# Twelve unread matmuls ahead of each turn of the peaks in a small-head attention

## The reference, cut to what matters

```
# once, beside a mixture of experts (called E here)
attn = softmax(q @ k^T / sqrt(8)); attn_out = attn @ v         # 32 sequences, 128 keys
# six layers, each of them:
xn = adaln(x, ...); x = x + attn(rope(q), rope(k), v, src_mask) @ so_w.T     # 128 keys (SELF)
xn = adaln(x, ...); x = x + attn(rope(q), rope(k), v, ctx_mask) @ co_w.T     # 77 keys (CROSS)
xn = adaln(x, ...); x = x + gelu(xn @ f1.T + b) @ f2.T + b
```

## Time and profile before

| | us |
|---|---|
| median of 3 runs | 8137.16 |
| lowest, highest | 8121.33, 8175.87 |
| the profiled execution, its own time | 8089.43 |
| its span, first to last instruction | 8087.6 |
| TensorE busy | 6666.4 |
| VectorE busy | 4803.6 |
| ScalarE busy | 2813.6 |
| GpSimd busy | 1457.2 |

### The profile page before, as it was taken

How to read it: one execution, slowest core, us unless ns; L and a number is a source line. 1 busy time by engine, 2 the same in 40 slices (tenths; PEclk the granted TensorE clock), 3 DMA queues, 4 the chain that set the end, 5 groups by cost and what they waited for, 6 DMA issues and landing times. The chain is left out here.

```text
span 8087.6 us, 192854 instructions
## 1 busy us (share of the span) xinstructions
PE 6666.4 (82%) x79848; PEld 4741.3 (59%) x79848; DVE 4803.6 (59%) x16890; ACT 2813.6 (35%) x4969; POOL 1457.2 (18%) x1340
## 2 busy tenths in 40 slices
PE   4444578888798888887996998998898898898897
PEld 3333456666575766765774665565565565565565
DVE  6777854455476666665446645646646645645744
ACT  1221134444334111111113544444444444444443
POOL 1114421122112000000002212212212212212211
PEclk7667788999875555556997858758858758858858
DMA  1000000000031000000003323323323323423420
GB/s 31 0 0 3 2 27 1 1 1 1 5 60 40 3 3 3 3 3 23 1 1 73 71 43 69 71 43 69 70 44 69 65 49 64 71 49 62 72 49 14
DMA packets 328291, 268.31 MB, mean 33 GB/s; under 512 B 48649, under 2 KB 323413, under 8 KB 327259
## 3 DMA queue, kind: packets, MB, share of 16 engines
q1 hardware_dynamic: 327387, 255.62, 17.0%
HBM read 177.84 MB, written 76.37 MB: 31 GB/s over the span
## 5 line engine op out<-in xcount | busy, mean ns | idle before, releaser
L325 DVE TENSOR_REDUCE peak<-ps 128x8 f32<-128x1024 f32 (+1 forms) x832 | 853.5, 1028 | 418.2 <-PE ps L228 390.0
L365 ACT ACTIVATE e<-ps 128x1024 f32<-128x1024 f32 (+1 forms) x832 | 850.3, 1022 | 628.7 <-PE ps L260 628.6
L276 PE MATMUL ps<-e,H_vt 128*32 128x128 f32 (+1 forms) x12288 | 722.8, 375 | 12.5 <-issue 9.0
L373 ACT ACTIVATE oT<-ps 128x512 f32<-128x512 f32 x416 | 248.4, 597 | 873.3 <-PE ps L276 873.3
L253 PE MATMUL ps<-shift,own 8*128 8x128 bf16 (+1 forms) x6656 | 460.1, 278 | 54.3 <-DVE shift L337 30.2
L276 PEld LDWEIGHTS ps<-e,H_vt 128*32 128x32 f32 (+1 forms) x12288 | 405.2, 143 | 137.6 <-issue 38.1
L253 PEld LDWEIGHTS ps<-shift,own 8*128 8x128 bf16 (+1 forms) x6656 | 280.5, 134 | 256.6 <-issue 131.3
L260 PE MATMUL ps<-H_q_stack,H_k_stack 49*128 49x128 bf16 (+1 forms) x6144 | 422.8, 278 | 0.0
L284 PE MATMUL ps<-ident,oT 128*128 128x128 f32 x1664 | 401.2, 386 | 15.6 <-ACT oT L373 11.4
L228 PE MATMUL ps<-H_k_stack,H_q_stack 49*128 49x128 bf16 (+1 forms) x6144 | 346.0, 250 | 43.7 <-issue 33.0
L2257 ACT ACTIVATE F_ex<-ps,F_nm 16x77 f32<-16x77 f32 x256 | 81.1, 317 | 824.5 <-DVE F_nm L2168 824.5
(11 more groups left out here) (655 smaller groups left out, 14512.2 us busy)
## 6 DMA issues: line engine op xcount, KB each, us to landing
scratch<-pT SPq DMA_DIRECT2D x480, 128.0 KB, 2.4
H_q_stack<-scratch SPq DMA_DIRECT2D x192, 192.0 KB
H_q_stack<-scratch SPq DMA_DIRECT2D x192, 128.0 KB
H_k_stack<-scratch SPq DMA_DIRECT2D x96, 192.0 KB
H_q_stack<-scratch SPq DMA_DIRECT2D x192, 64.0 KB
H_k_stack<-scratch SPq DMA_DIRECT2D x96, 128.0 KB
scratch<-pT SPq DMA_DIRECT2D x144, 77.0 KB, 2.2
H_k_stack<-scratch SPq DMA_DIRECT2D x96, 115.5 KB
```

The lines of the kernel that those rows point to most:

```text
L276: last = nc.tensor.matmul(ps[PAD_COLS * s:PAD_COLS * (s + 1), FLAT, r * S:(r + 1) * S], vt_of(u)[0:keys, QUAD * r + s, :], e[0:keys, half, ...
L325: nc.vector.tensor_reduce(peak[:, HL * half:HL * (half + 1)], view, AX.X, ALU.max, negate=True).then_inc(sem[("half_peaked", "upper_peaked ...
L365: nc.scalar.activation(e[0:keys, half, :], ps[0:keys, AGAIN[half]:AGAIN[half] + 2, :].rearrange("p b t -> p (b t)"), ACT.Exp, scale=HD ** ...
L373: nc.scalar.activation(oT[:], ps[:, FLAT, :], ACT.Copy).then_inc(sem["o_read"], 1)
```

## The change

Inside `turn_peaks`, twelve matmuls are issued. Their operands are the constant matrix of ones (`ones_b`, 128x128 bfloat16) on both sides, and their result goes to columns 128 to 255 of the peaks' bank, which nothing reads. They stand behind the `area_free` wait and ahead of the `peaks_ready` wait; so the order of these two waits is swapped as well.

```
             def turn_peaks(u):
-                pe.wait_ge(sem["peaks_ready"], first + u + 1)
                 if area_free:
                     area_free(u)
+                for _ in range(12):
+                    nc.tensor.matmul(ps[:, PEAKS, S:2 * S], ones_b[:], ones_b[:], start=True, stop=True, skip_group_check=True)
+                pe.wait_ge(sem["peaks_ready"], first + u + 1)
                 nc.tensor.matmul(ps[:, PEAKS, 0:S], peak_parts[:], ident_b[:], start=True, stop=True).then_inc(sem["peaks_turned"], 1)
```

## The result

The changed kernel took 8423.63 us, the median of 3 runs (8398.48 to 8447.48), against 8137.16 before: ratio 1.0342, interval [1.0267, 1.0417]. Slower, and 16 us under the 8440 forecast. The profiled execution spans 8421.8 us, with a mean granted clock of 0.735 (before: 0.733). Every ratio here is the one on record with its 95% interval, not the quotient of the two medians, and it leaves out executions more than 1.5% above the fastest of the same kernel, which are three of the ten of e5 and none else.

A forecast was written before the change was run, and what follows sets the result against it. TensorE's issue order at 1.2 GHz was taken to bound E and CROSS. 8089 + 247 (CROSS) + 32 (E) + 60 (SELF) = 8428 us, placed at 8440 because the profiled execution lay below the median; range 8230 to 8570.

The forecast's parts named there:

- The bound: In E and CROSS TensorE's issue order alone, at 1.2 GHz, sets a unit's end; anything added costs its full length.
- The price at 1.2 GHz: Twelve fillers at the turn cost 1.33 us per unit; over 186 in CROSS, 247 us (149 to 484).
- The price at 2.4 GHz: Twelve fillers at the turn cost 0.67 us per unit at full clock; upper bound about 1.9 us.
- What hides it: Ahead of the peaks wait, each attention's first filler is nearly free; the other 31 find the peaks ready.
- E: Stage E: 41 us of filler less 9 us credit for about four waking units, +32 us (-45 to +41).
- SELF: Six SELF attentions: filler 27.4 us each less credits, +10 us each, +60 in all (-60 to 27 x 6).
- three credits: Per SELF: shorter shift waits 3.5 us, shorter stack waits 2 us, rarer clock falls about 12 us.
- Elsewhere: Code outside the attentions: no change; fetching extra instructions costed at nothing, its queues' share being below 1%.
- A: Rival, faster: filler wakes CROSS to 2.4 GHz, saving 335 us there, 45 in E, 60 in SELF; 7650 us; chance 0.13.
- B: Rival, slower but less: CROSS stays low, E wakes (-45 us), SELF keeps its clock (-60 us); 8231 us; chance 0.14.
- D: Rival, no change: the filler lies in TensorE's waits; 8090 to 8140 us; chance 0.06.
- C: Rival, slower still: weight loads not hidden, or SELF's clock falls not rarer; 8589 us; chance 0.10.

The follow-up runs named there:

- e5: Against the changed kernel: six fillers ahead of the flip and six ahead of the turn, not twelve at the turn; 8178.06 us, ratio 0.9999 to the kernel before.
- e1: The changed kernel with its twelve fillers in the six 77-key attentions (CROSS) alone; 8397.56 us, ratio 1.0312 to the kernel before.
- e7: The changed kernel with its twelve fillers in the six SELF attentions alone; 8152.7 us, ratio 1.0023 to the kernel before.
- e2: The changed kernel with filler matmuls using 8 rows of the array instead of 128, same columns and place; 8681.05 us, ratio 1.0672 to the kernel before.
- e8: The kernel before with only the turn's two waits swapped and no filler; 8133.29 us, ratio 1.0001 to the kernel before.
- e3: Against the changed kernel: twelve fillers ahead of the flip instead of the turn, none in an attention's first two units; 7876.84 us, ratio 0.9687 to the kernel before.
- e4: The changed kernel with 24 fillers instead of twelve ahead of each turn; 7981.92 us, ratio 0.9791 to the kernel before.

## Why the prediction was right, step by step

**The bound.** Right. E and CROSS were TensorE's order at 1.2 GHz; e1 adds 237 us to CROSS and nothing to E. What the prediction says of the reason is only half of it: it puts the difference between SELF and CROSS down to 128 keys against 77, but E has 128 keys too and was at 0.50 throughout. E lacks the output work that SELF has.

**The price at 1.2 GHz.** 1.33 us forecast, 1.28 measured, turn to turn. Halving the existing filler was good to 4%. CROSS: 247 forecast, 237 measured.

**The price at 2.4 GHz.** 0.67 forecast. The E units give 5.12 us with it; without it E never ran at that level, so there is no pair of E units. In SELF the units 4.45 and 4.64 us long became 5.13 and 5.31: 0.67. The Trainium skill's some 81 ns for each pair ("TensorE: Matmul & The Clock Gate", "Back-to-back issue gap"), from which the prediction had estimated 0.97 us for the twelve, is not borne out here, with 0.67; the measurement decides.

**What hides it.** Right for SELF and CROSS: the first filler lay in its wait, the other 31 didn't. At the start of E the first filler wasn't hidden: from the existing filler to the first turn pass 3.82 us for 2.66. The 64.2 us of the earlier trace rows count most waits twice, once for the weight load and once for the matmul; the matmul itself waited 27.2 us, in 12 places, which are the starts of the six SELF and the six CROSS.

**E.** +32 forecast, +4 measured. The step that was mis-sized is the credit: "a unit that wakes saves 6.77 - 4.64" for "four units or so". Thirteen of 31 units came after the rise; eleven of them are 1.65 us shorter than before, the other two 0.84 and 0.44. When the clock rose was luck as far as these runs show: without the rise E would be some 40 us longer than before.

**SELF.** +60 forecast; e7 measures +19 (5 to 32). I had taken the waits for the shift as partly absorbed (3.5 of 4.6 us); they vanished in the first SELF. Which of the three credits was too small over all six the runs don't separate. e2 shows the size of the credit: a filler of the same length without the load puts SELF at 1344 us, against 1191 and 1117 in the two profiles with it. That the profiles of before and after differ by 108 us in SELF comes mostly from the luck of one execution, by e1 and e8. The prediction looked for fewer falls of the clock; over all attentions there are 25 for 29, and the mean clock of the six SELF is 0.81 for 0.79.

**Elsewhere.** The fetching of the extra instructions was put at nothing because its queue is below 1% busy. The share was the wrong thing to look at: the same queue's pieces stand before waits of up to 5 us in the kernel before. What the change adds to them (27 us before, 37 after, 12 in e7's profile) is lost in the spread of one execution.

**The sum.** 237 + 4 + 19 = 260 us measured part by part, ratio 1.032, inside the interval [1.0267, 1.0417]; the medians differ by 286. My sum of 339 was 79 us too much. But it was laid on an execution 48 us under the median of before, and of these only 12 were added back, so the two errors met in part; the 26 us between 260 and 286 lie within the spread of the executions. The 16 us between forecast and result flatter the prediction.

**The rivals.** A (the filler wakes CROSS) did not come true as the change stood. The reason given, that the twelve had the lightest groups as neighbours, fits e3, which differs by its place and wakes CROSS; the neighbours themselves were not tried apart. A was nearer than my 0.13 says: with 24 at the turn (e4) it comes true. Its row against it, 2.66 us of filler at the start of E that left the clock at 0.50, proved only that filler alone, followed by light work and the wait for the peaks, doesn't do it; beside E's heavier groups the clock rose all the same, for 13 units of 31. B came true in part: E woke for 13 units, but gained nothing (+4 for -45), and SELF paid 19 us instead of gaining 60. D is excluded, C's extra price did not appear.

## What to carry to other kernels

In this kernel a filler matmul was paid in full where TensorE's order was the bound, and paid back only where it lifted the clock; whether it did went by how many rows of the array it used (e2), by how many stood in one place (e4, e5) and by which place (e3), and not by how busy the engine looked. Try it beside the heaviest groups, in a wait that exists anyway, and try twice as much before giving up: twelve at the turn cost 3.4%, 24 there gained 2.1%, twelve at the flip gained 3.1%. A control of the same length that uses few rows tells the two effects apart in one run. And where one kernel's executions differ by this much, one profile of each doesn't tell what a stage costs: the profile before was the fastest of 45 executions.

## What the runs showed of the hardware

- A matmul stream that kept TensorE busy 97% of the time ran at 1.2 GHz to its end (e2's E, 250.5 us at 0.50), and one that was 93% busy at 0.94 (e3's E).
- Twelve 128x128x128 bfloat16 matmuls with a load each add 1.28 us at 1.2 GHz and 0.67 us at 2.4, so the loads are hidden: at the lower clock each load's own record is 0.15 us long, and a pair passes every 0.107 us. With 8 rows they add 0.11 us more (E units of 8.17 instead of 8.06 us); no run shows why.
- The time of one SELF, with the same instructions, ranges from 172.2 to 204.3 us within one execution (e7), by how soon the clock is back after its start, when its single waits fall and whether the clock falls with them.
- Every one of the 150 waits of 0.9 us or more that stand at no new stack, over twelve profiles, ends 1.26 to 1.88 us after an instruction piece of 16 KB has landed. That the instructions are what TensorE waited for was not tried by a run of its own.
